# Reordering a GpSimd queue between row scatters and a square root, and one VectorE instruction with it

## The reference

```python
x = x + tanh(g_xattn[1]) * attention1(layernorm(x), ctx)      # softmax attention, one head
x = x + tanh(g_ffn[1]) * experts1(layernorm(x))               # below
...
logits = einsum('bsd,de->bse', x, Wg)                         # 8 experts
top_vals, top_idx = top_k(logits, 2)
probs = softmax(top_vals)
# out += probs of expert e * ((silu(x @ W1[e]) * (x @ W2[e])) @ W3[e])
```

## Time and profile before

| | |
|---|---|
| median of 3 runs | 1051.98 us (1050.65 to 1052.35) |
| the profiled execution | 1050.65 us, its span 1048.4 us |
| mean granted TensorE clock over the span | 0.900 of full speed |
| the third phase | about 497 to 741 us of the span |

### The profile page before, as it was taken

How to read it: one execution, slowest core, us unless ns; L and a number is a source line. 1 busy time by engine, 2 the same in 40 slices (tenths; PEclk the granted TensorE clock), 3 DMA queues, 4 the chain that set the end, 5 groups by cost and what they waited for, 6 DMA issues and landing times. The chain is left out here.

```text
span 1048.4 us, 25663 instructions
## 1 busy us (share of the span) xinstructions
PE 806.5 (77%) x7841; PEld 586.2 (56%) x7841; DVE 677.9 (65%) x2651; ACT 514.3 (49%) x1099; POOL 452.8 (43%) x454
## 2 busy tenths in 40 slices
PE   1799999999986899996766666662588888788820
PEld 1466666666654466664545445442477777677720
DVE  3588888888887578885766666544244444444445
ACT  1477777777765455551544444431344444444400
POOL 1345363544540111110267777667255545555430
PEclk9899999999999699999887888855799989999965
DMA  4401001010000000001011111112222222222259
GB/s 110 132 20 34 22 18 35 18 35 18 18 2 3 0 1 0 0 1 52 23 49 54 56 53 54 48 39 77 62 73 78 73 66 73 73 71 78 68 167 339
DMA packets 57727, 57.46 MB, mean 55 GB/s; under 512 B 10261, under 2 KB 49709, under 8 KB 57677
## 3 DMA queue, kind: packets, MB, share of 16 engines
q1 hardware_dynamic: 40013, 34.28, 11.0%
q0 software_dynamic: 8640, 17.84, 4.8%
q10 hardware_dynamic: 9024, 4.73, 1.5%
HBM read 32.80 MB, written 24.02 MB: 54 GB/s over the span
## 5 line engine op out<-in xcount | busy, mean ns | idle before, releaser
L1598 POOL DMA_INDIRECT contributions<-d_y,d_token x142 | 135.9, 957 | 134.2 <-DVE d_y L1638 90.6
L1245 POOL DMA_INDIRECT sorted_rows<-r_send,r_slots x128 | 125.5, 980 | 45.1 <-issue 43.1
L1619 DVE COPY d_xT<-d_tr 128x256 f32<-128x256 f32 x71 | 30.1, 424 | 135.6 <-PE d_tr L1695 59.0
L1658 ACT ACTIVATE d_silu<-d_u 128x512 f32<-128x512 f32 x71 | 42.4, 597 | 140.6 <-PE d_u L1687 99.7
L1687 PE MATMUL d_u<-d_xT,d_w 128*128 128x256 f32 x284 | 79.4, 403 | 41.3 <-DVE d_xT L1619 31.6
L465 POOL TENSOR_SCALAR a_k_heads<-a_kT,head_of_group 128x512 f32<-128x512 f32 x60 | 93.0, 1566 | 2.7 <-ACT a_kT L510 2.7
L388 DVE TENSOR_REDUCE a_neg_max<-a_scores 128x16 f32<-128x1024 f32 x64 | 78.2, 1222 | 14.0 <-PE a_scores L619 12.5
L646 PE MATMUL a_probsT_bank<-ident,a_probs 128*128 128x128 f32 x512 | 80.8, 281 | 2.2 <-ACT a_probsT L541 0.3
L541 ACT COPY a_probsT<-a_probsT_bank 128x512 f32<-128x512 f32 x128 | 74.9, 585 | 11.4 <-PE a_probsT_bank L646 11.3
L534 ACT ACTIVATE a_probs<-a_scores 128x1024 f32<-128x1024 f32 x64 | 65.6, 1025 | 29.4 <-PE a_scores L629 29.3
L1687 PEld LDWEIGHTS d_u<-d_xT,d_w 128*128 128x128 f32 x284 | 50.0, 197 | 51.6 <-issue 26.0
(11 more groups left out here) (205 smaller groups left out, 1856.5 us busy)
## 6 DMA issues: line engine op xcount, KB each, us to landing
d_rows<-sorted_rows SPq DMA_DIRECT2D x71, 130.0 KB
d_pair<-contributions SPq DMA_DIRECT2D x16, 512.0 KB, 7.0
X<-in_x SPq DMA_DIRECT2D x16, 256.0 KB, 3.0
out_x<-X ACTq DMA_DIRECT2D x16, 256.0 KB, 7.4
ctxT<-in_ctx_T SPq DMA_DIRECT2D x16, 192.0 KB, 3.0
c_ctxT<-in_ctx_T SPq DMA_DIRECT2D x16, 192.0 KB
contributions<-d_y,d_token POOLq DMA_INDIRECT x142
w<-in_L_ffn_W SPq DMA_DIRECT2D x2, 1024.0 KB
```

The costliest lines, as they stand in the source:

```text
L1245: pool.indirect_dma_start(dispatch.rows, bass.IndirectOffsetOnAxis(ap=slots[par][:, k, j:j + 1], axis=0), send[par][k][:, j, :], None).the ...
L1598: pool.indirect_dma_start(dispatch.contributions, bass.IndirectOffsetOnAxis(ap=token[u % 2][:, h:h + 1], axis=0), shares[u % 2][:, h, :], ...
```

## The change

GpSimd's step sent the four scatters of k = 0, then did the second normalisation's power, then the four scatters of k = 1, then the first normalisation's power. Now it sends all eight scatters, then does the two powers one after the other. On VectorE the instruction that adds the epsilon for the second normalisation moves from just after the statistics to behind the choice of experts, in the same step. The number of instructions is unchanged.

```diff
             def step(g, par):
-                sent = group_now(g, 5)
-                if sent is not None:
-                    scatter(sent, 1 - par, (0,))
+                n = group_now(g, 5)
+                if n is not None:
+                    scatter(n, 1 - par, (0, 1))
                 n = group_now(g, 3)
                 if n is not None:
                     ln2.deviation(pool, n)
-                if sent is not None:
-                    scatter(sent, 1 - par, (1,))
                 n = group_now(g, -2)
                 if n is not None:
                     ln.deviation(pool, n)
...
                     wait_alone(dve, x_updated, n + 1)
                     ln2.statistics(dve, n)
-                    ln2.add_eps(dve, n)
                 r = group_now(g, 4)
                 if r is not None:
...
                     dve.tensor_tensor(chosen[:, 0:GT, :], top.first, top.second, ALU.add).then_inc(chosen_ready, 1)
+                n = group_now(g, 3)
+                if n is not None:
+                    ln2.add_eps(dve, n)
                 n = group_now(g, -1)
                 if n is not None:
                     ln.rows(dve, n, xn_transposed)
```

## The result

The changed kernel took 1066.49 us (median, 1063.74 to 1073.32), the kernel before 1052.16 us (1050.65 to 1052.66) beside it. The ratio is 1.0128, with a 95% interval from 1.0079 to 1.0177: about 14 us slower, where 13.2 us faster was forecast. The profiled execution took 1062.21 us with a span of 1060.4, which is 12.0 us more than before.

The account below looks back on a forecast made before the run. The third phase was taken as bound by VectorE's waits for scatters to land; 13.6 us leaves the chain, the phase shortens 13.2, so 1050.65 - 13.2 = 1037.4, plus 1.33 gives 1038.8 us, range 1033.5 to 1045.

Parts of the forecast that it names:

- the first part: Third phase, GpSimd: taking `r_rstd` out from between the scatters saves 1.0 us plus its idle time per step.
- the 13.6 us taken out: Third phase: seven rounds of scatters at 1.0 us plus 6.56 us of idle time ahead of the power leave the chain.
- the 12.87 us: Third-phase chain: rows pass through ScalarE, TensorE and VectorE from the buffer write to `c_variance`; part of the 27.43 us sum.
- the pair: Two successive third-phase steps, one stalled at line 1355 and one not; 27.4 us, forecast to become about 26.0.
- The stall at line 1355: VectorE waits for scatters to land before writing send buffers; 23.6 us in 9 pieces, forecast to fall to about 10.
- The idle time for `c_variance`: GpSimd waiting in the third phase before `c_rstd`; forecast to shrink from 2.33 us to about 1, covering the moved power.
- The idle time for `r_variance`: GpSimd waiting before `r_rstd` in the third phase; charged 6.7 us in the list of waits, forecast nearly gone.
- The epsilon's own cost of zero: VectorE's epsilon instruction moved behind the choice: hidden, cost zero; at most 0.17 us in each of 16 steps, 2.7 us.
- The one of the other sign, the clock that stays down: Rival, chance 0.07: TensorE's clock stays slow in each pair's second step, pair 28.7 us, time about 1054.5 us.
- the closed chain: Third-phase loop from line 1355's write through `c_variance`, powers and scatters to the next stalled write; 27.43 us per pair.
- the first rival: Chance 0.15: shorter stalls keep TensorE's clock up, GpSimd bounds a pair at 25.3 us, 3.5 us more gained, about 1035.
- the third rival: Chance 0.12: stall changes its name, VectorE waiting for `r_rstd` or GpSimd for `r_variance`, or tail gives back; about 1046.8 us.

Follow-up runs that it names:

- D: Comparison on chip 5 where signals came late: kernel before 1053.56 us, changed kernel 1065.24 us, ratio 1.0119.
- five then three: Against the kernel before: five scatters, the second normalisation's power, three scatters, epsilon at its old place; 1053.9 us, ratio 0.9981.
- B: Comparison on chip 0 where signals came late: kernel before 1062.07 us; GpSimd's new order alone 1079.01 us, ratio 1.0195.
- E: Comparison on chip 0 where signals came on time: kernel before 993.05 us; changed kernel with unused power between the fours 994.52 us, ratio 1.0005.
- A: First comparison, signals late: kernel before 1052.16 us, changed kernel 1066.49 us, ratio 1.0128.
- C: Comparison on chip 8 where signals came on time: kernel before 991.69 us, changed kernel 979.99 us, ratio 0.988.

## Why the prediction was wrong, point by point

**The step that failed** is in the first part: `r_rstd` between the scatters was entered as a pure cost of 1.0 us and its idle time, and of the 13.6 us taken out it said "All of it should arrive: GpSimd has no other place in a stall step that can hold the scatters up". The power was also a pause in a row of DMA instructions, and where TensorE's signals are late that pause lets them through. With it taken out the routing product's and the transposes' increments come 3.4 to 5.5 us late in each step from 564 to 657 us, about when the row of eight is over. In the sum the term is the 12.87 us from the write at line 1355 to `c_variance`, which was kept as it was: in the changed kernel's step it is 14.38 (604.21 to 618.59), 3.51 of it VectorE's wait behind the ended product. And each step has it now, so two steps take 31.4 us where the pair took 27.4. Order alone brings the late signals, and a power that computes nothing takes most of them away, in the same comparison as the changed kernel (3 of 3 us and more against 25): that is the test that shows it. Why the signals are held isn't shown.

The trace of before held a clue. In it the signals of line 1484 at 561 and 589 us are 0.77 us late behind the fourth scatter, and others up to 2.53, with rows of four. I didn't read the semaphore events against the ends of the matmuls.

**What came as forecast.** Scatters in unbroken eights, 8.93 + 0.96 = 9.9 us from the first start to the last end (9.85 forecast). The stall at line 1355 shrank, though not for the forecast's reason: not by 13.6 us but by all of its 23.6, since every step got longer than the landing needs. The idle time for `c_variance` is about 1 us a step (9.2 in 9). The idle time for `r_variance`, which was to vanish, is 22.9 us in 10 waits, 7.2 of it in one wait before the first scatters, which the kernel has where signals are on time too. For the rest, the epsilon now stands behind the choice, the choice waits for the routing product, and so the variance is late with TensorE's signal. The epsilon's own cost of zero was not tested by itself, since alone it meets the old order.

**The rivals.** The one of the other sign, the clock that stays down, doesn't explain the result. The clock did fall, from 0.77 to 0.71 over the third phase. But in D the kernel with five then three had 0.71 over the same phase too (497 to 745.1), and was level with before. So a phase at 0.71 does not by itself bring the loss; what share of the 14 us the lower clock carries was not separated. That a wait which leaves TensorE idle lowers its clock is the rule of the Trainium skill, "TensorE: Matmul & The Clock Gate", section "HAM oscillation"; by that rule, the trace agrees, and the price that I gave it (1054.5 us) would still be 12 us short of the time.

**Where the signals are on time** the forecast's size nearly held: 11.7 us faster (979.99 against 991.69) where 13.2 was said. The mechanism did so in part, so that far the nearness is luck. Line 1355 waits 0.2 to 0.3 us, so the closed chain was broken. What bounds the step next is GpSimd, 12.3 us a step (541.07 to 590.10, four steps), which I had only in the first rival (25.3 us for a pair; the first pair was 24.59), and VectorE waits for `r_rstd`, the new name that the third rival gave the stall. A trace of the kernel before from that comparison doesn't exist, so the 11.7 us can't be laid out row by row.

**What stays open.** Why one comparison has late signals and another not. It need not be the chip: B, with late signals, and E, without, carry the same chip number, if that number names the same chip; anything else that changed between the times at which they ran may be it. Every run was recorded, so whether the recording takes part isn't known. Whether the results of TensorE or only its signals come late. Whether a pause must be long or must be a certain instruction to free them, and why some increments deep in a row are not held. And which part of the 53 us in the fourth phase is theirs.

**A version that beats both kernels** everywhere was not found. Where signals are late, the changed kernel with the unused power is 0.5% faster than before, and with a pause behind each four writes of the fourth phase 1.1%. Where they are on time the changed kernel itself is best, 1.2% faster, and both of these are level or slower (1.0005 to 1.0031, and 1.0189). The kernel to ship depends on which of the two kinds of run it will meet, and nothing here foretells that.

## What to carry to other kernels

An instruction between DMA issues is not only its own time: where one row of GpSimd's indirect DMAs is made longer, look at what waits for TensorE during it, and compare its matmuls' ends with the starts of their readers. A wait put down to "remote" or "issue" behind a producer that has ended may be such a signal. A change worth one per cent should be timed in more than one comparison, beside the kernel before each time: here the same two kernels gave 1.2% faster and 1.2% slower.

## What the runs showed of the hardware

- TensorE's increments of semaphores reached the trace 0.01 to 0.05 us after the modelled end of the matmul while no indirect DMAs ran. In four of six comparisons up to 29 of a phase's came 3.0 to 6.1 us after it when they fell due in an unbroken row of more than five of GpSimd's indirect DMAs of 128 rows (24 in the changed kernel in A, 3.1 to 5.5 us, where before had none); in the other two comparisons they did not, with the same instructions. VectorE's increments were mostly spared (22 of 332 more than 0.1 us late, none more than 1.6).
- A power of 1.04 us in the middle of the row took most of that lateness away (3 of 3 us and more against 25); a nop (28), a memset of 0.12 us (29) and one of 0.54 us (18) did not.
- The same kernel before took from 991.69 to 1062.07 us (medians) in six comparisons. Between the traces of the changed kernel in A and C, the third phase begins with the same instruction at 491.0 and 492.0 us; it is over at 758.8 and 723.9, and the fourth takes 301.6 and 251.5 us. So nearly all of the difference is in the third and fourth phases, in which GpSimd sends rows.
